# One-hot routing rows turned by SBUF-to-SBUF transposing transfers, in a macaron block on one core

## The reference

```python
x = x + 0.5 * ffn(layernorm(x), Wr, W1, b1, W2, b2)
x = x + attn(layernorm(x), Wq, Wk, Wv, Wo)
x = x + 0.5 * ffn(layernorm(x), Wr, W1, b1, W2, b2)
```

```python
probs = softmax(x @ Wr); topk_probs, topk_experts = top_k(probs, 2)
pos = position of the token in its expert's queue; keep = pos < 40
buf[e, b, pos] += x * keep
y = relu(buf @ W1[e] + b1[e]) @ W2[e] + b2[e]
out = sum over the two choices of y[e, b, pos] * keep * prob
```

## Time and profile before

| | |
|---|---|
| median of 3 executions | 205.8 us (203.78 to 209.26) |
| the profiled execution's own time | 204.59 us |
| its span, first to last instruction | 202.8 us |
| PE busy | 185.0 us, 91% |
| ACT busy | 154.8 us, 76% |
| DVE busy | 145.0 us, 72% |
| POOL busy | 68.5 us, 34% |
| the chain that ended last | 76% on PE, 9% DVE, 5% ACT, 4% DMA |

### The profile page before, as it was taken

The page is one execution under the profiler, slowest core; times in us unless marked ns, Lnnn a source line. Parts: engine busy times, 40 slices in busy tenths (PEclk is TensorE's granted clock), DMA queues, the critical chain, the costliest instruction groups (busy, mean ns, idle before and its releaser), DMA issues.

```text
span 202.8 us, 6049 instructions
## 1 busy us (share of the span) xinstructions
PE 185.0 (91%) x2329; PEld 145.4 (72%) x2329; DVE 145.0 (72%) x408; ACT 154.8 (76%) x361; POOL 68.5 (34%) x104
## 2 busy tenths in 40 slices
...
GB/s 149 313 331 315 14 5 0 0 3 3 0 3 130 173 217 274 120 131 202 218 205 6 228 201 197 121 94 0 3 0 3 0 3 0 3 2 28 81 3 103
DMA packets 21741, 19.69 MB, mean 97 GB/s; under 512 B 1704, under 2 KB 18640, under 8 KB 21712
## 3 DMA queue, kind: packets, MB, share of 16 engines
q1 hardware_dynamic: 21568, 19.29, 35.2%
...
q10 hardware_dynamic: 144, 0.00, 0.0%
...
## 4 chain that ended last, share of the span: by engine, by line
PE 76%; DVE 9%; ACT 5%; DMA 4%; issue 2%; SPq 1%; POOL 1%; DVEq 0%; ACTq 0%; POOLq 0%
PE psB L992 16%; PE psB L1062 8%; PE psS L1045 6%; PE psS L869 4%; PE psB L879 4%; PE psS L870 4%; PE psS L871 4%; PE psB L968 3%; PE psB L1064 3%; ACT amat L630 3%; DMA stack<-qk_parts 3%; DVE oh L782 2%; PE psB L928 2%; PE psB L1083 2%; PE psB L950 2%
## 5 line engine op out<-in xcount | busy, mean ns | idle before, releaser
L549 POOL TENSOR_SCALAR_AFFINE_SELECT amat<-amat 128x512 f32<-128x512 f32 x64 | 44.0, 692 | 49.1 <-ACT amat L630 48.1
L630 ACT ACTIVATE amat<-psS 128x768 f32<-128x768 f32 x64 | 49.9, 815 | 6.8 <-PE psS L1047 5.8
L601 ACT ACTIVATE hid<-psS,biasT 128x160 f32<-128x160 f32 x128 | 39.7, 401 | 10.0 <-PE psB L992 5.8
L992 PE MATMUL psB<-hid,w 128*128 128x160 f32 x256 | 40.3, 305 | 0.0
L992 PEld LDWEIGHTS psB<-hid,w 128*128 128x128 f32 x256 | 35.5, 190 | 0.7 <-DVE xTf L725 0.3
L869 PE MATMUL psS<-xe,w 128*128 128x160 f16 x128 | 27.2, 233 | 0.7 <-ACT hid L601 0.3
L870 PE MATMUL psS<-xe,w 128*128 128x160 f16 x128 | 27.2, 233 | 0.0
L871 PE MATMUL psS<-xe,w 128*128 128x160 f16 x128 | 27.2, 233 | 0.0
L1045 PE MATMUL psS<-stack 64*128 64x256 f16 x128 | 17.1, 278 | 3.7 <-ACT amat L630 2.0
L1062 PE MATMUL psB<-amat,vst 128*32 128x256 f32 x256 | 20.4, 390 | 0.0
L1045 PEld LDWEIGHTS psS<-stack 64*128 64x128 f16 x128 | 6.2, 93 | 14.0 <-issue 5.6
...
## 6 DMA issues: line engine op xcount, KB each, us to landing
qk_parts<-qk SPq DMA_DIRECT2D x16, 256.0 KB, 3.8
stack<-qk_parts SPq DMA_DIRECT2D x16, 256.0 KB, 3.8
stack<-qk_parts SPq DMA_DIRECT2D x32, 128.0 KB, 3.8
amat<-in_L_ffn_W SPq DMA_DIRECT2D x8, 256.0 KB, 5.7
w<-in_L_ffn_W SPq DMA_DIRECT2D x8, 256.0 KB, 5.7
x<-in_L_attn_hidden_states SPq DMA_DIRECT2D x4, 256.0 KB, 4.5
out<-x SPq DMA_DIRECT2D x8, 128.0 KB, 1.9
amat<-in_L_attn_Wq SPq DMA_DIRECT2D x1, 128.0 KB, 4.6
```

Source lines behind the costliest of these rows:

```text
L549: pool.affine_select(out=d, in_=d, pattern=[[0, 2], [0, 2], [1, P]], compare_op=ALU.is_ge, fill=0.0, base=0, channel_multiplier=-1).then_i ...
L601: ins = act.activation(hid[:, n % 2, c, :], psS[:, wide_slot(s) + c // 2, (c % 2) * GS:(c % 2 + 1) * GS], ACT.Relu, bias=biasT[:, e * HC + ...
L630: act.activation(amat[:, n % A_RING, :, :], psS[:, wide_slot(s):wide_slot(s) + 2, 0:T + P], ACT.Square)\
L992: ins = mm(bank(s)[:, 0:GS], w2[:, e, c, :], hid[:, n % 2, c, :], start=(c == 0), stop=(c == HC - 1))
```

## The change

The stage `ot` leaves PE, ACT and DVE. It is now a stage of SP, `ot.l.g.h`, for half a unit (h = 0, 1): one transposing transfer that reads four tiles of `oh`, 128x1536 fp16 or 384 KB, and writes 12 turned blocks of 128x128 into `ohT`, whose layout changes to fit. Two per unit, eight in all. Each has the semaphore `turned[h]`; a transfer waits for the `oh` compares of its half, for the earlier transfer of its half, and in layer 1 for the last `cb` that read the part of `ohT` that it overwrites. `cb`, `ca` and the rewriting of `oh` wait for `turned` where they waited for a bank. All four tables are rewritten.

```diff
-             ("ot", 1, 0), ("v", 1), ("v", 2), ("v", 3), ("v", 6), ("v", 7),
+             ("v", 1), ("v", 2), ("v", 3), ("v", 6), ("v", 7),
 PE_STAGES (two lines of each):
-yt.0.0.1 yt.0.0.2 pw.0.1 down.0.1.1 up.0.1.3 cb.0.0.0 cb.0.0.1 up.0.1.4 cb.0.0.2 cb.0.0.3 down.0.1.2 up.0.1.5
-down.0.1.3 down.0.1.4 xt.1.0 up.0.1.6 qk.0.0.0 qk.0.0.1 qk.0.1.0 qk.0.1.1 v.0 ot.0.1.0 up.0.1.7 v.1 ot.0.1.1
+up.0.1.3 down.0.1.2 up.0.1.4 cb.0.0.2 cb.0.0.3 xt.1.0 up.0.1.5 qk.0.0.0 qk.0.0.1 qk.0.1.0 qk.0.1.1 down.0.1.3
+down.0.1.4 up.0.1.6 pw.0.1 yt.0.1.0 v.0 down.0.1.5 up.0.1.7 v.1 down.0.1.6 down.0.1.7 xt.1.1 yt.0.1.1 yt.0.1.2
 SP_STAGES (the new ones whole):
+ot.0.0.0 ot.0.0.1 qk.0.0.0 qk.0.0.1 ot.0.1.0 qk.0.1.0 qk.0.1.1 ld.0 ld.1 qk.1.0.0 qk.1.0.1 qk.1.1.0 ot.0.1.1
+qk.1.1.1 ld.2 ld.3 qk.2.0.0 qk.2.0.1 qk.2.1.0 qk.2.1.1 ld.4 qk.3.0.0 qk.3.0.1 ld.5 qk.3.1.0 qk.3.1.1 ld.6 ld.7
+ot.1.0.0 ot.1.0.1 ot.1.1.0 cb.1.0.0 cb.1.0.1 cb.1.0.2 cb.1.0.3 ot.1.1.1 cb.1.1.0 cb.1.1.1 cb.1.1.2 cb.1.1.3
 macaron_program:
-        ohT = sb("ohT", [P, 2, GB, KT, T], f16)
+        ohT = sb("ohT", [P, 2, GB * TT, KT, P], f16)
+        turned = [sem(f"turned{c}") for c in range(2)]
+        def wait_turned(eng, l, g, i):
+            eng.wait_ge(turned[2 * i // GB], 16 * (units.index((l, g)) + 1))
 SP:
+                elif s[0] == "ot":
+                    _, l, g, h = s
+                    u = units.index((l, g))
+                    if u == 0:
+                        sp.wait_ge(consts_made, 2)
+                    else:
+                        sp.wait_ge(turned[h], 16 * u)
+                    if l:
+                        wait_ready(sp, ("cb", l - 1, g, GB - 1))
+                    sp.wait_ge(oh_ready, GB * u + 2 * h + 2)
+                    rows = slice(h * GT // 2, (h + 1) * GT // 2)
+                    sp.dma_start_transpose(ohT[:, parity(l, g), rows, :, :].rearrange("p t k c -> p (t k) c"),
+                                           oh[:, parity(l, g), rows, :].rearrange("p t s -> p (t s)")).then_inc(turned[h], 16)
 DVE, stage ps (rewriting oh):
-                        wait_ready(dve, ("ot", s[1] - 1, s[2], GB - 1))
+                        wait_turned(dve, s[1] - 1, s[2], 0)
+                        wait_turned(dve, s[1] - 1, s[2], GB - 1)
 PE:
-                            ins = mm(dst[:, t * P:(t + 1) * P], ohT[:, parity(l, g), i, k, t * P:(t + 1) * P],
+                            ins = mm(dst[:, t * P:(t + 1) * P], ohT[:, parity(l, g), TT * i + t, k, :],
-                elif kind == "ot":
-                    i = s[3]
-                    m16 = bank16(s)
-                    for k in range(KT):
-                        for t in range(TT):
-                            o = (k * TT + t) * P
-                            last = pe.transpose(m16[:, o:o + P], oh[:, parity(*s[1:3]), TT * i + t, k * P:(k + 1) * P], ident16[:, :])
 ca (all four sequences of the last unit) and cb:
-                        wait_taken(pe, ("ot",) + s[1:3] + (i,))
+                        wait_turned(pe, *s[1:3], i)
-                    wait_taken(pe, ("ot", l, g, i))
+                    wait_turned(pe, l, g, i)
```

More of the change, by code:

```diff
@@ L79 @@
 PE_STAGES = stages("""
[L80 to L84, removed]
@@ L95 @@
[L95 to L99, removed]
@@ L100 @@
[L100 to L103, removed]
+wc rx.0 rx.1 rl.0 rl.1 warm.6.0 warm.30.1 warm.10.2 ps.0.0 dph.0.0.0 dpl.0.0.0 dph.0.0.1 dpl.0.0.1 dph.0.0.2
@@ new lines @@
+bt dpl.0.0.2 dph.0.0.3 dpl.0.0.3 warm.8.3 up.0.0.0 up.0.0.1 xt.0.2 down.0.0.0 up.0.0.2 down.0.0.1 up.0.0.3
+lg.0.1.0 xt.0.3 up.0.0.4 lg.0.1.1 down.0.0.2 up.0.0.5 down.0.0.3 up.0.0.6 ps.0.1 down.0.0.4 down.0.0.5
+up.0.0.7 dph.0.1.0 dpl.0.1.0 dph.0.1.1 dpl.0.1.1 down.0.0.6 dph.0.1.2 dpl.0.1.2 dph.0.1.3 dpl.0.1.3 pw.0.0
+yt.0.0.0 yt.0.0.1 down.0.0.7 up.0.1.0 yt.0.0.2 up.0.1.1 down.0.1.0 up.0.1.2 cb.0.0.0 cb.0.0.1 down.0.1.1
+up.0.1.3 down.0.1.2 up.0.1.4 cb.0.0.2 cb.0.0.3 xt.1.0 up.0.1.5 qk.0.0.0 qk.0.0.1 qk.0.1.0 qk.0.1.1 down.0.1.3
@@ new lines @@
+sc.7.5 sc.7.6 ox.6 sc.7.7 dph.1.0.1 dpl.1.0.1 dph.1.0.2 oT.6 dpl.1.0.2 av.7.1 av.7.2 av.7.3 dph.1.0.3
+dpl.1.0.3 wo.6 ox.7 up.1.0.0 xt.2.2 oT.7 wo.7 up.1.0.1 up.1.0.2 down.1.0.0 down.1.0.1 up.1.0.3 up.1.0.4
+lg.1.1.0 xt.2.3 down.1.0.2 lg.1.1.1 down.1.0.3 up.1.0.5 down.1.0.4 up.1.0.6 down.1.0.5 ps.1.1 up.1.0.7
+down.1.0.6 dph.1.1.0 down.1.0.7 dpl.1.1.0 dph.1.1.1 dpl.1.1.1 pw.1.0 dph.1.1.2 dpl.1.1.2 dph.1.1.3 dpl.1.1.3
+yt.1.0.0 yt.1.0.1 up.1.1.0 yt.1.0.2 up.1.1.1 down.1.1.0 up.1.1.2 down.1.1.1 up.1.1.3 down.1.1.2 up.1.1.4
@@ L110 @@
[L110 to L114, removed]
@@ L120 @@
[L120 to L124, removed]
@@ L125 @@
-down.1.1.7 yt.1.1.1 yt.1.1.2 yt.1.1.3
+rx.0 ln1.0.0 rx.1 ln1.0.1 w1.0 w1.1 nm.0.0 nm.0.1 w1.2 w1.3 ln1.0.2 dph.0.0.0 wr w1.4 dpl.0.0.0 dph.0.0.1
+dpl.0.0.1 dph.0.0.2 dpl.0.0.2 dph.0.0.3 bt dpl.0.0.3 up.0.0.0 ln1.0.3 up.0.0.1 up.0.0.2 down.0.0.0 w1.5 w1.6
+down.0.0.1 up.0.0.3 ex.0.0 w1.7 up.0.0.4 down.0.0.2 down.0.0.3 up.0.0.5 up.0.0.6 down.0.0.4 down.0.0.5
+dph.0.1.0 dph.0.1.1 up.0.0.7 down.0.0.6 dph.0.1.2 dph.0.1.3 ex.0.1 yt.0.0.0 down.0.0.7 up.0.1.0 yt.0.0.1
+yt.0.0.2 sq.0 up.0.1.1 down.0.1.0 up.0.1.2 ln1.1.0 wqkv down.0.1.1 down.0.1.2 up.0.1.3 up.0.1.4 qk.0.0.0
@@ new lines @@
+qk.0.0.1 qk.0.1.0 qk.0.1.1 ln1.1.1 down.0.1.3 up.0.1.5 down.0.1.4 up.0.1.6 up.0.1.7 yt.0.1.0 down.0.1.5
+down.0.1.6 v.1 down.0.1.7 yt.0.1.1 yt.0.1.2 qk.1.0.0 qk.1.0.1 qk.1.1.0 qk.1.1.1 sc.0.0 sc.0.1 sc.0.2 sc.0.3
+ln1.1.2 v.2 sc.0.4 sc.0.5 v.3 sc.0.6 sc.0.7 sc.1.0 sc.1.1 ln1.1.3 xe.0.0 xe.0.1 sc.1.2 sc.1.3 qk.2.0.0 sc.1.4
+qk.2.0.1 qk.2.1.0 sc.1.5 sc.1.6 sc.1.7 xe.1.0 qk.2.1.1 sc.2.0 sc.2.1 xe.1.1 sc.2.2 sc.2.3 oT.0 sc.2.4 sc.2.5
+sc.2.6 sc.2.7 sc.3.0 oT.1 sc.3.1 sc.3.2 qk.3.0.0 qk.3.0.1 sc.3.3 sc.3.4 sc.3.5 ln1.2.0 v.6 xe.3.0 sc.3.6
```

74 lines of the change are left out of this document (33 added, 41 removed).

## The result

The changed kernel took 206.85 us in the median of 18 executions (205.06 to 208.57), the kernel before beside it 205.47 (203.39 to 209.26). The ratio is 1.009, 95% interval 1.0055 to 1.0124: slower by about 1.9 us (1.1 to 2.5), clear of zero but less than 2% (4.1 us). 206 us was forecast. The profiled execution took 206.74 us.

The account below looks back on a forecast made before the run. PE was taken to bound the expert units, with loads ahead of the first scores. Terms -2.4 + 4.0 - 2.7 + 1.5 = +0.4 us, on a median of 205.8, gave 206 us, range 199.5 to 217 us.

Parts of the forecast that it names:

- What is removed: Layer 1's two units: PE loses their transposes, 1.35 us a unit, so a gain of 2.7 us.
- qk.0 sooner by 5.0 us: Ahead of the first queries and keys: PE loses transposes and stages moved behind, so these come 5.0 us sooner.
- ot.0.1.0: Transfer between second and third store of qk.0: delays the last store, first scores at 73.7 us, gain 2.4 of 4.4 us.
- L: Delay of qk.0's last store: 1.5 us of issue plus 1.2 us behind 384 KB of data, 2.7 us.
- Ti: Time SP is held to issue one transposing transfer: 1.5 us taken, 0.6 low end, 3 us high end.
- T: Transposing transfer from issue to landing: 5 us behind other transfers, 4 us where quiet; 1.9 low, 8 us high.
- The serial case: Rival for every transfer: crossing goes block by block, 15.7 us each, total 235 us and more; chance 0.13.
- ot.0.1.1, 4.0 us: At cb.0.1.2 in the attention: PE stalls 4.0 us for the transfer issued behind three stores of qk.1.
- I take it whole: At cb.0.1.2: the 4.0 us stall counts fully, as the rest of the attention and SP's ld.2 stand behind it.
- ot.1.1.1, 1.5 us: At the end, ahead of ca: transfer behind unit (1, 0)'s stores stalls PE 1.5 us, with nothing behind to absorb it.
- The orders, 1 us either way: Attention stages in the rewritten tables: differ from before by a few stages, worth 1 us in either direction.
- about no change: Whole kernel: outcome with transfers landing in 2.8 to 6.5 us, own range 202 to 210 us; chance 0.38.

## Why the prediction was right

The number was right to 1 us, with luck: two of its terms were wrong by some 4 us each, in opposite directions. By its own steps:

- **What is removed**, 2.7 us in layer 1: 2.4 us (53.2 to 50.8). Right.
- **qk.0 sooner by 5.0 us.** PE's first product of it moved from 60.4 to 56.0 us, 4.4. Nearly right; then **ot.0.1.0** behind two stores: the issue took 1.59 us, the last store 4.35 us to land instead of 3.18, 1.2 us more, the very two terms of L. The first scores came at 74.37 us instead of 73.7, a gain of 1.7 for 2.4.
- **The price of a transfer.** Ti 1.53 us for 1.5, T 4.3 us for 4 to 5. The bound by 256-byte packets named the right packets and priced them too high: the queue's 12544 further packets took 43.7% of 205.0 us less 35.2% of 202.8 us, times 16 engines, by which I estimate 23 ns each for 53. The serial case is out.
- **ot.0.0.x, ot.1.0.x and ot.1.1.0 hidden**: no wait for any of them. Right.
- **ot.0.1.1, 4.0 us.** The wait was 4.42 us, and that it is so near is luck. T was 7.24 us there, not 5, and above the 6.5 us that the prediction had named as a sign of being wrong. The issue alone held SP for 4.17 us, although it began 1.7 us after the first scores and not 2.4. PE came later too, 4.65 us after the first scores instead of 3.4, since its two `cb` had taken 2.69 us at the lower clock; at full clock it is there after 3.00 us, and the wait is 6.1 (6.13 us with `ot.0.1.0` moved, 6.07 with `ot.1.1.1` moved, where the clock did not fall ahead of it). The second step that failed is "I take it whole": what follows the wait was in no term. In the attention's length the place cost 7.8 us: `cb.0.1.2` 6.1 us later, then 2.0 us for the work at about half the clock (4.67 us, for 2.64 with `ot.0.1.1` moved), less 0.3 that the rest of the attention took back. In time it cost 7.4.
- **ot.1.1.1, 1.5 us.** "It waits for both halves" was wrong: `ca` waits sequence by sequence, and did two of them (1.1 us) while the second half was on its way. The wait was 1.30 us with T = 5.3, and the lower clock behind it cost the 32 last products 1.4 us in the profiled execution, 2.7 us together; by the timed runs the place cost 1.9 us. Near in time, for partly other reasons.
- **The orders, 1 us either way.** This is the third step that failed, by 4.2 us of gain in the attention. I had compared which stages stand ahead of which milestone, and found little; the sequence inside was what counted. The row that would have told was in the trace of before: 7.3 us of waits for `amat` ahead of the scores.

So the sum reads, in the profiled execution: -1.7 at the first scores, -4.2 by the attention's order, +7.8 at `cb.0.1.2`, -2.4 in layer 1, +2.7 at the end (205.0 - 195.3 against 202.8 - 195.8), together +2.2, which is the 202.8 us before and the 205.0 after. Against +0.4 forecast, the two errors of +3.8 and -4.2 all but cancel, which is luck, and the smaller ones (0.7, 0.3 and 1.2) leave 1.8 us. The forecast of "about no change" holds; its account of why does so only in part.
